# Gated cross-attention and quantised feed-forward on one core: the probability-times-value product in three fp16 parts, with the value projection ahead of the output product and both score maxima at the front of VectorE's step

## The reference

```
q, k, v = layernorm(x) @ Wq, ctx @ Wk, ctx @ Wv        # 256 -> 1024 each
p = softmax(causal_and_mask(q k^T / 8))                # per batch element and head, 128 x 128
x = x + tanh(g_xattn) * ((p v) @ Wo + bo)
x = x + tanh(g_ffn) * down(qdq(silu_qdq(gate) * up))   # of layernorm(x), weights in 4-bit blocks of 32
```

## Time and profile before

| | us |
|---|---|
| median of 3 runs | 1624.89 (1622.98 to 1626.07) |
| the profiled execution | 1626.47 |
| its span, first to last instruction | 1624.6 |
| TensorE busy in the span | 1530.6 (94%) |
| VectorE busy | 1385.1 (85%) |
| ScalarE busy | 1253.4 (77%) |
| GpSimd busy | 1033.8 (64%) |

### The profile page before, as it was taken

How to read it: one execution, slowest core, us unless ns; L and a number is a source line. 1 busy time by engine, 2 the same in 40 slices (tenths; PEclk the granted TensorE clock), 3 DMA queues, 4 the chain that set the end, 5 groups by cost and what they waited for, 6 DMA issues and landing times. The chain is left out here.

```text
span 1624.6 us, 38058 instructions
## 1 busy us (share of the span) xinstructions
PE 1530.6 (94%) x12556; PEld 1251.8 (77%) x12556; DVE 1385.1 (85%) x2247; ACT 1253.4 (77%) x3222; POOL 1033.8 (64%) x1004
## 2 busy tenths in 40 slices
PE   7899999999999999999999999789989997995998
PEld 5787887877877878878778788677767776775887
DVE  7888888888888888888888889878887998998996
ACT  5887887888778778878887787566758998885674
POOL 3988988888888889888888888600006664740000
PEclk9999999999999999999999999999998999997999
DMA  6554445444444544454444445369957884755664
GB/s 195 118 127 103 105 106 122 104 92 115 106 105 103 126 102 105 107 121 104 92 115 106 105 103 98 86 205 344 321 215 262 282 287 153 276 227 187 218 214 145
DMA packets 347365, 252.23 MB, mean 155 GB/s; under 512 B 287792, under 2 KB 317616, under 8 KB 344368
## 3 DMA queue, kind: packets, MB, share of 16 engines
q1 hardware_dynamic: 347312, 251.58, 55.1%
HBM read 105.25 MB, written 76.02 MB: 112 GB/s over the span
## 5 line engine op out<-in xcount | busy, mean ns | idle before, releaser
L496 ACT ACTIVATE prob<-masked,neg_max 128x128 f32<-128x128 f32 x1024 | 397.6, 391 | 35.1 <-DVE neg_max L662 31.6
L431 POOL TENSOR_TENSOR prob_parts<-prob,prob_parts 128x512 f16<-128x512 f32 x254 | 310.3, 1241 | 2.7 <-ACT prob_parts L504 1.6
L426 POOL TENSOR_TENSOR prob<-prob,scaled 128x512 f32<-128x512 f32 x256 | 271.6, 1061 | 20.1
L660 DVE TENSOR_TENSOR masked<-score,mask_add 128x512 f32<-128x512 f32 x256 | 174.6, 682 | 74.0 <-PE score L963 67.9
L504 ACT ACTIVATE prob_parts<-prob 128x512 f16<-128x512 f32 x254 | 159.0, 627 | 75.6 <-POOL prob L426 71.7
L496 ACT ACTIVATION_READ_ACCUMULATOR prob<-masked,neg_max 128x1 f32 x1024 | 193.3, 189 | 0.0
L662 DVE TENSOR_REDUCE neg_max<-masked 128x4 f32<-128x512 f32 x256 | 175.6, 686 | 8.8
L438 POOL TENSOR_TENSOR probT<-turn 128x512 f32<-128x512 f16 x125 | 173.2, 1386 | 0.0
L1723 POOL TENSOR_SCALAR xThi<-n_x 128x1024 fp32r<-128x1024 int16 x15 | 43.8, 2919 | 202.9 <-DMA n_x<-n_x_d 166.8
L976 PE MATMUL y<-wo_hi,o_hi 128*128 128x256 f32 x508 | 148.3, 292 | 15.9 <-DVE o_lo L667 15.2
L424 POOL TENSOR_TENSOR scaled<-rsums,pscale 128x4 f32<-128x4 f32 x256 | 66.4, 259 | 124.0 <-DVE rsums L654 123.9
(11 more groups left out here) (249 smaller groups left out, 4485.5 us busy)
## 6 DMA issues: line engine op xcount, KB each, us to landing
gate<-gate_d SPq DMA_DIRECT2D x30, 768.0 KB, 4.3
n_x<-n_x_d SPq DMA_DIRECT2D x25, 512.0 KB, 4.9
gate_d<-stage SPq DMA_DIRECT2D x8, 1536.0 KB, 5.5
n_u_d<-w_raw SPq DMA_DIRECT2D x16, 768.0 KB, 4.1
stage<-n_u_d SPq DMA_DIRECT2D x16, 768.0 KB, 6.0
gate_d<-gate SPq DMA_DIRECT2D x7, 1536.0 KB, 5.5
x_in<-in_x SPq DMA_DIRECT2D x16, 512.0 KB, 3.9
ctx_in<-in_ctx_columns SPq DMA_DIRECT2D x16, 512.0 KB, 4.8
```

What stands on the lines that cost most here:

```text
L426: gp.tensor_tensor(prob[:, h], prob[:, h], scaled[:, h, :].rearrange("p (b o) -> p b o", o=1).broadcast_to([P, NB, P]), ALU.mult).then_inc ...
L431: gp.tensor_tensor(prob_parts[:, h, 1], prob[:, h].rearrange("p b k -> p (b k)"), prob_parts[:, h, 0], ALU.subtract).then_inc(prob_low, 1)
L496: nc.scalar.activation(prob[:, h, b, :], masked[:, h, b, :], ACT.Exp, bias=neg_max[:, h, b:b + 1], accum_out=psums[:, h, b:b + 1]).then_in ...
L660: nc.vector.tensor_tensor(masked[:, h], score[h][:], mask_add[:], ALU.add).then_inc(masked_done, 1)
```

## The change

- `v` is no longer kept in fp32. ScalarE writes its fp16 high part and VectorE the fp16 low part, for all 8 value projections of a group (before, each engine copied four of them). Both scale by `v_mul`, made from a bound on the values: VectorE takes the largest magnitudes of each context row (`ctx_top`, step 6) and once of the weights (`w_top`), TensorE multiplies them (`value_bound`, two fp32 matmuls of one column, step 7), and VectorE makes the scale (`value_scale`, end of step 7). The residual takes the scale out again (`output_unit`, one small operation in step 4).
- The turned fp16 parts go to the value product as they are: high x high, high x low and low x high, 24 fp16 matmuls a step instead of 8 fp32 ones. `join_prob` and `join_second` go away, and the transposing transfer now waits for the value product instead of for them.
- TensorE does the value projections before the output product.
- VectorE does both heads' maxima first, then `o_lo`. Its value part stands between background work and head 1's reciprocals.
- GpSimd's `add_bias` moves from step 6 to step 0 of the next group, ahead of the probabilities.
- In the first three steps and after the last group the order is fitted to this; the last unit's probabilities are now split by ScalarE and VectorE.

The core of the diff:

```
@@ gpsimd step
-                if old:
-                    join_second(u - 3, (c + 1) % 2, NC // 2 * g + (c - 1) // 2)
+                if c == 0 and not (isinstance(g, int) and g == 0):
+                    add_bias(g - 1)
...
@@ scalar
+            def values_high(g, i, n):
+                b, before = nth(g, i)
+                if n == 0:
+                    act.wait_ge(v_scaled, 4 * g + 3)
+                act.wait_ge(projected[b], before + 1)
+                nc.scalar.activation(v16[:, n % NB, n // NB, 0], proj[b][:], ACT.Copy, scale=v_mul[:, 0:1]).then_inc(v_high, 1)
...
                 if soft:
                     exps(u - 1, 0)
-                if new:
+                if new and not early:
                     copy_k(g, c, u)
+                for i, n in vs[:1]:
+                    values_high(g, i, n)
...
                 if soft:
                     exps(u - 1, 1)
...
+                for i, n in vs[1:]:
+                    values_high(g, i, n)
                 if soft:
                     high_prob(u - 1, 0, c % 2, NC // 2 * g + c // 2)
...
@@ vector
+            def values(g, jobs):
+                for i, n in jobs:
+                    b, before = nth(g, i)
+                    dve.wait_ge(v_high, NC * g + n + 1)
+                    nc.vector.scalar_tensor_tensor(v16[:, n % NB, n // NB, 1], proj[b][:], v_mul[:, 0:1], v16[:, n % NB, n // NB, 0],
+                                                   ALU.mult, ALU.subtract).then_inc(copied[b], 1)
+
+            def ctx_top(g):
+                dve.wait_ge(ctx_loaded, 16 * (g + 1))
+                nc.vector.tensor_reduce(c_top[:], ctx_in[:], X, ALU.max, apply_absolute_value=True).then_inc(v_scaled, 1)
...
                 if soft:
                     maxima(u - 1, 0)
+                    maxima(u - 1, 1)
                 if oldest:
                     attended_low(u - 4)
-                if old:
-                    join_prob(u - 3, 0, (c + 1) % 2, NC // 2 * g + (c - 1) // 2)
                 if soft:
-                    maxima(u - 1, 1)
                     reciprocals(u - 1, 0)
...
+                if c == 4:
+                    output_unit(g)
+                if c == 6 and more:
+                    ctx_top(g + 1)
...
+                if new:
+                    values(g, vs[:1])
                 if soft:
                     reciprocals(u - 1, 1)
-                if c < 3:
-                    values(g, c)
+                if new:
+                    values(g, vs[1:])
+                if nxt:
+                    value_scale(g + 1)
                 if c == 4 and after_first:
                     second_moments(g - 1)
...
+            dve.wait_ge(w_loaded[5], 16)
+            nc.vector.tensor_reduce(w_top[:], w_stage(2), X, ALU.max, apply_absolute_value=True)
+            ctx_top(0)
             w_low_part(3)
             drive(dve, step)
...
@@ tensor
                 for b in range(NB):
...
-                    for h in range(2):
-                        last = nc.tensor.matmul(pv[h * HD:(h + 1) * HD, b, :], v_sb[:, b, c * P + h * HD:c * P + (h + 1) * HD],
-                                                probT[:, h, b, :], start=True, stop=True)
+                    for n, (m, t) in enumerate(((0, 0), (0, 1), (1, 0))):
+                        for h in range(2):
+                            at = c % NB * P + h * HD
+                            last = nc.tensor.matmul(pv[h * HD:(h + 1) * HD, b, :], v16[:, b, c // NB, m, at:at + HD],
+                                                    turn[:, slot, h, t * NB + b, :], start=(n == 0), stop=(n == 2))
...
+            def value_bound(g):
+                pe.wait_ge(v_scaled, 4 * g + 1)
+                for k in range(KC):
+                    last = nc.tensor.matmul(trans[:, 0, 0:1], c_top[:, k:k + 1].broadcast_to([P, P]), w_top[:, k:k + 1],
+                                            start=(k == 0), stop=(k == KC - 1))
+                last.then_inc(v_bound, 1)
...
                 if nxt:
                     transpose_in(g, *ts[0])
+                if first or fourth:
+                    pe.wait_ge(w_ready, 3 if first else 6)
+                if new:
+                    for i, n in jobs_of(c, "v"):
+                        value(g, i, n)
                 if oldest:
...
                     out_product(u - 4, (c - 4) % NC)
                 if nxt:
                     transpose_in(g, *ts[1])
-                if first or fourth:
-                    pe.wait_ge(w_ready, 3 if first else 6)
-                if new:
-                    for i, n in jobs_of(c, "v"):
-                        value(g, i, n)
+                    value_bound(g + 1)
                 if old:
-                    times_v(u - 3, co, (g, c, u) if new else None)
+                    times_v(u - 3, co, (c + 1) % 2, NC // 2 * g + (c - 1) // 2, (g, c, u) if new else None)
```

More of the change, by code:

```diff
@@ L130, in attention @@
         kT = sb("kT", [P, T])
-        v_sb = sb("v_sb", [P, NB, INNER])
+        v16 = sb("v16", [P, NB, 2, 2, VH], F16)
+        v_stage = v16[:].rearrange("p b h n i -> p (b h n i)").bitcast(F32).rearrange("p (b i) -> p b i", b=NB)
+        w_top, c_top = sb("w_top", [P, KC]), sb("c_top", [P, KC])
+        v_unit, v_mul, y_unit = (sb(n, [P, 1]) for n in ("v_unit", "v_mul", "y_unit"))
         masked = sb("masked", [P, 2, NB, P])
@@ L202, in attention @@
         xres_loaded = sem("xres_loaded")
-        probT_copied = [sem(f"probT_copied{h}") for h in range(2)]
+        v_high = sem("v_high")
+        v_scaled = sem("v_scaled")
+        v_bound = sem("v_bound")
+        last_turned = sem("last_turned")
         pv_done = sem("pv_done")
@@ L432, in low_prob, with add_bias @@
                                  ALU.subtract).then_inc(prob_low, 1)
[L434 to L439, removed]
+            def add_bias(g):
+                gp.wait_ge(xres_loaded, 16 * (g + 1))
+                gp.tensor_tensor(xres[:], xres[:], bo_g[:].rearrange("p (o n) -> p o n", o=1).broadcast_to([P, NB, D]),
+                                 ALU.add).then_inc(xres_ready, 1)
             def step(g, c):
                 u, new, soft, old, more = parts(g, c)
-                if old:
-                    join_second(u - 3, (c + 1) % 2, NC // 2 * g + (c - 1) // 2)
                 if c == 3 and new and more:
@@ L449, in step @@
                         make_rstd2(g - 1)
[L450 to L453, removed]
+                if c == 0 and not (isinstance(g, int) and g == 0):
+                    add_bias(g - 1)
+                if c == 6 and new and not more:
+                    add_bias(g)
                 if soft:
@@ L532, in step @@
                     exps(u - 1, 1)
-                if isinstance(g, int) and g == 0 and c < 3:
+                if early and c < 2:
                     w_high_part(4 + c)
-                if new and c > 2:
-                    for i, n in jobs_of(c, "v"):
-                        b, before = nth(g, i)
-                        act.wait_ge(projected[b], before + 1)
-                        nc.scalar.activation(v_sb[:, n % NB, VH:2 * VH], proj[b][:], ACT.Copy).then_inc(copied[b], 1)
+                for i, n in vs[1:]:
+                    values_high(g, i, n)
                 if soft:
@@ L573, in _ @@
             attended(U - 2)
-            act.wait_ge(last_step, 1)
             act.wait_ge(pv_done, U - 1)
-            nc.scalar.activation(probT[:, 0], trans[:], ACT.Copy).then_inc(probT_copied[0], 1)
-            for n in range(4):
+            for h in range(2):
+                act.wait_ge(last_step, h + 1)
+                nc.scalar.activation(turn[:, 1, h, 0:NB], trans[:], ACT.Copy).then_inc(v_high, 1)
+                if h == 0:
+                    ffn_high_part(0)
+            for n in range(1, 4):
                 ffn_high_part(n)
@@ L937, in scores_free, with times_v @@
                     wait(pe, masked_done, 2 * (u - 1) + h + 1)
[L939 removed]
+            def times_v(u, c, slot, times, then=None):
                 for h in range(2):
[L943 removed]
+                    if times is None:
+                        pe.wait_ge(last_turned, 2)
+                    else:
+                        pe.wait_ge(prob_turned[h][slot], 16 * times)
                 wait(pe, out_split, u)
@@ L996, in step @@
                     weights_left(g, c, jobs_of(c, "k")[0][0], 1)
+                if first:
+                    value_bound(0)
                 if nxt:
                     transpose_in(g, *ts[0])
+                if first or fourth:
[3 more added lines that the diff above has]
+                        value(g, i, n)
                 if oldest:
```

84 lines of the change are left out of this document (44 added, 40 removed).

## The result

The changed kernel takes 1680.6 us (median of 4 runs, 1672.4 to 1687.7) where the kernel before took 1624.5 in the same series: the ratio is 1.034, 95% interval 1.030 to 1.039. Forecast were 1658 us, with 1620 to 1690 as the range and 0.82 for slower. The profiled execution has a span of 1677.8 us, 53.2 more than before.

The account below looks back on a forecast made before the run. TensorE was taken to bound the kernel, with little room behind it. +2.05 us a group gave +29 for groups 1 to 14; with the ends, +33.5 on 1626.5 made 1660 profiled, 1658 median, range 1620 to 1690.

Parts of the forecast that it names:

- The value product: TensorE's 24 fp16 records as 12 pairs at 0.06 us: 0.83 us instead of 1.02, saving 0.19 a step.
- Rival C: fp16 pairs of the value product as slow as fp32 ones, 0.11 us each: +38 us, 1697; chance 0.09.
- Plain steps: Steps paced by TensorE (1, 2, 3, 6): 7.44 us, -0.19 each, -0.8 a group.
- Rival A: VectorE enters steps 5 and 7 by t = 0.9, so all stalls go and TensorE's gain shows: 1587 us; chance 0.14.
- Rival B: Collisions with GpSimd vanish without its joins, 0.9 less in step 5, 0.7 in step 7: 1632 or 1627 us; chance 0.07.
- Step 4: Late residual delays the next qT copy, so the value projection starts 0.54 us late: 7.98 us, +0.35.
- Step 5: Moments end late, at t = 2.15, so the output product waits 1.4 us for `o_lo`: 8.8 us, +0.9.
- Step 0: The `o_lo` wait of 0.8 us goes, but value projections wait 0.4 and 0.8 for copies: +0.1.
- Step 7: Late layer norm delays `o_lo`, no value projection covers it: 9.1 us, +1.3, and +0.2 for another collision.
- the layer norm may be caught once more: VectorE's layer norm may meet another GpSimd operation: 0 to +0.7 us on step 7, taken as +0.2.
- Group 0: `w_top` and `ctx_top` ahead of the first scores +2.5 us, its step 7 +1.5, six steps -0.19: +3.
- Group 15 and the tail: Group 15 has steps 4 and 5 but no next columns: +0.5 us; tail has two more chain operations, fewer joins: +1.

Follow-up runs that it names:

- w2: w1 with the second value projection of step 0 behind the output product instead of in front; 1599.2 us, ratio 0.982.
- c2: Changed kernel with the layer norm ahead of head 1's reciprocals in step 6, the second norm's maximum behind them, `ctx_top` in step 2; 1638.0 us.
- w1: c2 with `o_lo` between the maxima in steps 5 and 7, step 3's residual behind head 1's reciprocals, `ctx_top` ahead of `w_top`, 28 idle transposes; 1612.8 us.
- b2: Kernel before with TensorE's order alone changed (value projection ahead of the output product), fp32 value product kept; 1641.6 us, ratio 1.009.
- c1: Changed kernel with 20 transposes of the identity filling TensorE's wait ahead of the output product in step 7; 1662.9 us, ratio 1.022.
- s1: Changed kernel with `w_top` and group 0's `ctx_top` over 4 columns a slice; one profiled run, first scores at 19.15 us instead of 25.63.
- a1: Changed kernel with VectorE's order alone as before, `o_lo` between the two heads' maxima; 1656.0 us, ratio 1.018.
- a3: Changed kernel with TensorE's and VectorE's orders both as before, so the fp16 value product and its value parts alone; 1719.4 us, ratio 1.057.
- d1: Changed kernel with the layer norm ahead of head 1's reciprocals in step 6 and the two maxima behind them, all staying in that step; 1656.5 us.
- b1: Kernel before with both TensorE's and VectorE's orders changed, fp32 value product, joins and value copies kept; 1684.2 us, ratio 1.036.

## Why the prediction was right in sign and short in size

- **The value product**: forecast 0.83, measured 0.79. With the prediction's 0.05 for the slow first and 0.12 behind the last, that is 11 intervals of about 0.056 us (an estimate), half of an fp32 pair. That is the lower bound given. The Trainium skill, "TensorE: Matmul & The Clock Gate", Back-to-back issue gap, has 81 ns for a sustained stream and about 56 for an isolated gap at 128 columns; for these pairs, which sit side by side in two column halves, the trace goes with the 56. Rival C falls.
- **Plain steps**: forecast 7.44, measured 7.34. Right, 0.1 better.
- **Rival A (no late chains)**: falls by the rows of steps 5 and 7. It was right on one thing: without late chains the kernel with the fp16 product is faster than the one before, as w2 shows with its other edits.
- **Rival B (no collisions)**: falls. `v_eps` and `vare` take 1.03 and 1.08, and the layer norm 2.93. The prediction prices the collisions gone at -18 us in its range and at -26 in this rival; the two don't agree.
- **Step 4**: forecast 7.98, measured 7.99, and the residual and both reciprocals within about 0.2 us of where the forecast had them. c2 has 7.99 and w1, with the residual behind the reciprocals, 7.55; what else w1 changes in the loop is in steps 5 and 7, so the residual is the likely cause, but it was not tried alone. b2 has the late output product too and stays at 7.61, so the lateness counts only together with the value parts.
- **Step 5**: forecast 8.8, measured 8.96. The moments ended at t = 2.39 (forecast 2.15), `o_lo` at 5.70 (forecast 5.5). The rows, as the earlier trace rows:

```profile
127.57 1.03 DVE L621 TENSOR_SCALAR v_eps<-v_sum 128x4 f32<-128x4 f32 x1
128.63 1.08 DVE L623 SCALAR_TENSOR_TENSOR vare<-m_sq,v_eps 128x4 f32<-128x4 f32 x1
129.64 0.68 DVE L671 TENSOR_TENSOR masked<-score,mask_add 128x512 f32<-128x512 f32 x1
```

- **Step 0**: forecast +0.1, measured 0.0 (mean).
- **Step 7**: forecast 9.3, measured 9.87 even with the clock up. The term that failed is "the layer norm may be caught once more: 0 to +0.7, I take +0.2". It was caught by a second GpSimd operation and took 2.93 instead of 2.09, 0.84 more, just above the upper bound. Its start, 7.0 into step 6, was as forecast.
- **The clock**: nowhere in the forecast. This is the largest miss: 14 us in groups 1 to 14 of the profiled execution, 18 between the medians of c1 and the changed kernel. A stall of 2.4 us was priced as 2.4 us. It also fits the scatter: the changed kernel's runs lie 15 us apart, with a mean clock of 0.970 in the shortest and 0.961 in the longest, while those of c1 lie within 5.
- **Group 0**: forecast +3, measured +9.6. The step that failed is "partly beside transfers": TensorE waited 5.4 us for the bound, then ran its value projections at the lower clock. s1 shows 5.0 of it up to the seventh scores. About 1.0 more is step 7. Most of the rest, 2.7 us, lies in step 3, which takes 12.05 where it took 9.38: the k projection waits 1.89 for a value's low part, and the slow clock follows. First the changed kernel, then c1 in the same place (TensorE's timeline and a stretch of each):

```profile
44.63 0.50 PE L927 MATMUL proj<-tc_hi,wk_hi 128*128 128x512 f32 x1 [1.89 <-DVE v L696]
48.00:50.00 2.00, 1.75 (x4) 1.49 (x5) 0.58 (x3) 1.94 (x10) 2.00 (x3) 0.50 0.38 72
```

```profile
43.60 0.50 PE L927 MATMUL proj<-tc_hi,wk_hi 128*128 128x512 f32 x1 [1.73 <-DVE v L696]
48.00:50.00 2.00, 2.00 (x44) 1.46 (x46) 1.18 (x2) 2.00 (x8) 2.00 (x3) 1.00 0.89 166
```

c1 has nearly the same wait, keeps the clock and takes 10.26 for the step. So about 1.8 of the 2.7 us goes with the clock here too. That is read from traces; no run changes it alone.

- **Group 15 and the tail**: forecast +0.5 and +1, measured -0.1 and -1.1 (from the last scores on). No run looks into that.

Added up for the profiled execution: 31 us for the steps of groups 1 to 14 (forecast 29), 14 for the clock, 9.6 for group 0, -1.2 for the rest. The late chains of steps 5 and 7 were there as forecast. The profiled time came out 20 us above the 1660 forecast for it; the clock in the loop (14) and group 0 (6.6 more than forecast) are that difference. The agreement of 31 with 29 is partly luck: step 7 was forecast 0.57 too short, 8 us in 14 groups, and the four plain steps 0.1 too long each, 6 us the other way. That 1680.6 lies within the range of 1620 to 1690 is in part luck too, for the clock had no term in it.

## What to carry to other kernels

Price an order of work step by step and by the engine that comes late into the step, not by busy shares: two kernels with the same instructions differ here by 25 us (a1), and two edits that cost 93 and 14 us alone (the fp16 product in a3, TensorE's order in b2) cost 30 together (a1). Where a forecast adds a stall of the size seen here, about 2 us, to TensorE, price the clock it comes back to as well. Background work that another engine's operations can stretch goes where that engine waits (d1), and work that isn't due yet goes out of the step that makes its engine late (`ctx_top` in c2).

## What the runs showed of the hardware

- In groups 1 to 14 TensorE's granted clock fell to its 1.2 GHz level behind stalls of 2.4 us (9 of 14 groups) and 2.1 us (b1, 10 of 14), and not behind stalls of 1.2 (a1) or 1.4 and 1.6 (d1). In step 3 of group 0 it fell with a stall of 1.9 us in the changed kernel and in d1, and not in a1 with the same stall. So the same stall gives either. It cost about 1.5 us each time in the loop (13.6 us in 9 groups).
- VectorE's layer norm operations (SBUF to SBUF, 256 columns) last 0.38 us at the least, 0.32 start to start, and up to 1.26 when they meet a GpSimd operation. A maximum over 1024 columns is not stretched: 1.19 to 1.22 beside GpSimd's operations in every group, 1.21 at the start (18.79 us), where GpSimd is idle. The Trainium skill, "SBUF — State Buffer", Who interferes with whom, has the port pair of the two as an exclusive lock which a `tensor_scalar` can ask for and a `tensor_reduce` never does on this chip; both agree with these rows.
- A one-column matmul with a 128-column weight is cheap: the four of `value_bound` take 0.43 us, start to start.
